# Routed expert blocks begun while the last two pairs of the graph part are still in their stages, and a pair of row blocks every three slots

## Chip, cores and metric

One Trainium2 chip, one NeuronCore of it. The metric is the device time of one execution in microseconds (us), median of the runs shown. Engines are called as in the profile: PE is TensorE, DVE VectorE, ACT ScalarE, POOL GpSimd, SP the SyncE queue.

## What is computed

6,250 nodes with 256 features, 206,250 directed edges sorted by destination. Two graph layers and a projection, then a mixture of 8 experts of which each node takes 2:

```
h6 = relu(segment_sum((ln(x) @ W6)[src] * norm, dst) + b6)
h7 = relu(segment_sum((h6 @ W7)[src] * norm, dst) + b7)
x  = x + h7 @ Wp + bp
xn = ln(ln(x)) * gamma + beta;  logits = xn @ Wr + br;  two largest, softmax weights w
y  = sum over the two experts e of w_e * (gelu(xn @ W1[e] + b1[e]) @ W2[e] + b2[e])
out = x + y
```

All arithmetic that the change touches is float32; `norm` comes from the summed edge weights of the two ends.

## The kernel before

**Layer 1** ends at about 1880 us of the span. Nothing in it is touched.

**Layer 2** runs over numbered slots, from one list that all engines follow (`layer2_slots`). The first 720 of the edge tiles are applied as 24 dense chunks of 3.3 MB, one chunk over four slots, so slots 0 to 95 hold dense matmuls (line 1722). The other tiles are 112 groups of 8, one group a slot in slots 0 to 111 (`L1_GROUPS`): POOL gathers eight times 128 rows with an indirect DMA (`gathers`, line 805) into a ring of four groups, PE sums them (`sums`, line 1736), ACT copies the sum (`copy_sums`, line 1443), PE combines it with the group before (`combine`, lines 1746 and 1748), ACT copies that (`copy_rows`), and SP stores it to `zsum`. POOL may not gather group n before PE has summed group n-4.

**Pairs.** The nodes lie in 25 pairs of 128-row blocks. When its sums are complete, a pair goes through four stages, one a slot (`pair_stage`, `stage_of`, `stage_first`, `stage_last`): stage 0 loads the sums (`zrow<-zsum`), scales and transposes them (lines 1143, 1756) and projects them (line 1768); stage 1 adds the residual and normalizes twice on DVE (`residual_and_norms`); stage 2 transposes (line 1781), computes logits (line 1791) and routes (`router`, with a tanh on ACT, line 1515); stage 3 ranks the rows by expert, works out each row's place in the list of its expert (`places`, its last instruction line 1224) and adds the second bias (line 1812; `first_output`, line 1228). `pair_starts` gives a pair its first slot; the next starts at least `PAIR_SLOTS` = 4 slots later, so no slot holds two pairs. The last starts are 93, 97, 101, 105, 109, 113 and 117; there are 121 slots.

**Sends.** POOL writes each pair's rows to their places in `sorted_x` with four indirect DMAs (`send`, line 813), one a slot, behind the gathers of that slot, 7 slots after the stage (`SEND_LAG`). Each waits until the one before has landed and until the pair is `placed`.

**Experts.** After the last pair has been sent, SP fills the ends of the experts' lists with padding (lines 770 to 774), DVE builds the list of 105 blocks of 128 rows (`block_table`), and the blocks follow one another (`experts`, `block_T`, `block_up`, `block_down`, `block_gelu`, `block_out`): SP loads the rows of block j (line 781), PE transposes them (line 1853), ACT scales (line 1549), DVE copies the block's weights out of the eight experts' (lines 1277, 1284), PE multiplies up (line 1863), ACT applies gelu (line 1559), PE multiplies down (line 1873), ACT weights the rows (line 1567), and POOL adds them to `acc` with an accumulating indirect DMA (line 852). That add waits for the landing of the add before:

```
for j in range(BLOCKS):
    pool.wait_ge(y_ready, j + 1)
    if j:
        pool.wait_ge(y_added, 16 * j)
```

PSUM results of blocks j and j+1 lie in two banks each (`ps_xe`, `ps_h`, `ps_y`). At last SP copies `acc` to the output.

Of the kernel before, what the change touches and what calls it, by code (L numbers as in the profile page):

```python
# [41 lines left out]
PAIR_SLOTS = 4  # L42
# [3 lines left out]
BLOCKS = 105  # L46
SEND_LAG = 7
# [29 lines left out]
def gnn_moe_kernel(nc, A):  # L77
# [32 lines left out]
    with ExitStack() as ctx:  # L110
# [54 lines left out]
        first_of = sb("first_of", [P, NE])  # L165
# [88 lines left out]
        def taker(first, last):  # L254
# [3 lines left out]
            def take(*shape):  # L258
# [8 lines left out]
                if len(shape) == 3:  # L267
# [35 lines left out]
        w2_sb = moe(NE, HC * D)  # L303
        w1_e = moe(2, KD, H)
# [12 lines left out]
        passed, jumps = (w1_e[:, i].rearrange("p k h -> p (k h)").rearrange("p (e j) -> p e j", e=NE)  # L317
                         for i in range(2))
# [34 lines left out]
        ps_b2 = split(bank[5][:, :], PT)  # L353
# [71 lines left out]
        LOADED = 10  # L425
        TABLE0_PARTS = X_LOADS
# [115 lines left out]
        STAGE_AT = {slot + s: (i, b, s) for i, (slot, b) in enumerate(STARTS) for s in range(PAIR_SLOTS)}  # L542

        def layer2_slots(f):

            for n in range(SLOTS):
                c, j = n // 4, n % 4
                f(n, c if c < CHUNKS else None, j, n if n < L1_GROUPS else None, STAGE_AT.get(n))
# [5 lines left out]
        def _(sp):  # L554
# [104 lines left out]

            bad = flag(sp)  # L660
            with sp.If(bad < 1):
# [43 lines left out]
                def layer2_slot(n, c, j, g, stage):  # L705
                    if stage and stage[2] == 0:
                        i, b, _ = stage
# [17 lines left out]
                    if stage and stage[2] == PAIR_SLOTS - 1:  # L725
                        store_acc(stage[0], stage[1])

                layer2_slots(layer2_slot)
            with sp.Else():
# [38 lines left out]
            sp.wait_ge(sent, 16 * 2 * PT * NPAIR)  # L768
            sp.wait_ge(pay0_made, 1)
            sp.dma_start(sorted_x[FILL:FILL + P, :], pay0[:, :]).then_inc(filled, 16)  # L770
            sp.wait_ge(counted, 1)
            for e in range(NE):
                end = sp.value_load(fill_i[0:1, e:e + 1], min_val=0, max_val=FILL)
                sp.dma_start(sorted_x[bass.ds(end, P), :], pay0[:, :]).then_inc(filled, 16)
# [1247 lines left out]
```

## Time and profile before

| | us |
|---|---|
| median of 3 runs | 3775.18 (3773.27 to 3778.09) |
| the profiled execution | 3771.15 |
| its span in the trace | 3769.3 |
| first gather of layer 2 | 1875.91 |
| last gather of layer 2 | 3129.72 |
| last pair placed | 3215.53 |
| first and last add of a block to `acc` | 3256.18 and 3742.8 |

Times of single instructions are counted from the start of the span. The profiled execution lies 4.0 us under the median and 1.9 us above its own span.

### The profile page before, as it was taken

To read this page: it belongs to the slowest core of one execution; us is meant where nothing else is said; L and a number is where in the kernel's file an instruction comes from. 1 tells how busy PE (TensorE), PEld (TensorE's weight loads), DVE (VectorE), ACT (ScalarE), POOL (GpSimd) and SP (SyncE) were. 2 spreads that over 40 slices of the span, in tenths; PEclk is the share of its full clock that TensorE was granted. 3 is DMA by queue.
4 is the path that set the end of the run, shared out by engine and by line. 5 is a ranking of instruction groups with operands and counts; after the bars stand their busy time and mean duration, and the time that the engine had idled before them with its cause. 6 is when DMAs were issued, how large, how long until landed. Compare 5 with 4: busy or idle time off the path is not lost.

```text
span 3769.3 us, 58587 instructions
## 1 busy us (share of the span) xinstructions
PE 2954.2 (78%) x17257; PEld 2010.3 (53%) x17257; DVE 1995.1 (53%) x7494; ACT 1383.3 (37%) x3705; POOL 1993.6 (53%) x2006
## 2 busy tenths in 40 slices
PE   4577289988999999996588888888988664588885
PEld 3456145555555555553355565555655422477775
DVE  7999886777676777751202333333433354333332
ACT  5577355555555555542301111111111110344443
POOL 0000177655555566666277777777777773233332
PEclk9979699999999999998889999888988765799998
DMA  3001355555445555557456666666666642233334
GB/s 102 0 18 36 90 168 164 163 162 164 152 135 162 161 164 165 162 175 232 121 166 211 202 202 200 202 200 201 197 200 201 214 124 72 56 58 58 58 58 106
DMA packets 208606, 535.63 MB, mean 142 GB/s; under 512 B 42924, under 2 KB 138436, under 8 KB 202052
## 3 DMA queue, kind: packets, MB, share of 16 engines
q0 software_dynamic: 105936, 263.26, 28.1%
q1 hardware_dynamic: 99796, 253.82, 19.3%
q10 hardware_dynamic: 2592, 15.16, 1.0%
q8 instruction: 131, 2.15, 0.2%
q14 instruction: 151, 1.24, 0.1%
HBM read 380.42 MB, written 158.05 MB: 143 GB/s over the span
## 4 chain that ended last, share of the span: by engine, by line
PE 38%; DVE 20%; DMA 16%; issue 10%; ACT 7%; POOL 6%; DVEq 2%; SPq 1%; ACTq 0%; POOLq 0%
PE bank L1722 15%; DMA acc<-arena 8%; PE bank L1714 6%; POOL arena L805 6%; DMA zrow<-zsum 5%; ACT arena L1452 3%; DVE arena L942 3%; PE bank L1748 3%; PE bank L1746 3%; PE bank L1736 2%; ACT arena L1460 2%; DMA zsum<-zc 2%; PE bank L1768 2%; PE bank L1863 2%; DVE arena L1112 1%
## 5 line engine op out<-in xcount | busy, mean ns | idle before, releaser
L805 POOL DMA_INDIRECT arena<-table,src_i x1792 | 1723.6, 962 | 843.2 <-issue 514.3
L1722 PE MATMUL bank<-arena 128*128 128x257 f32 x4704 | 1215.6, 394 | 5.5 <-ACT zcd L1469 5.5
L1722 PEld LDWEIGHTS bank<-arena 128*128 128x128 f32 x4704 | 876.7, 196 | 227.6 <-issue 103.4
L1460 ACT ACTIVATE arena<-arena 128x128 bf16<-128x128 bf16 x1440 | 482.4, 393 | 295.9 <-DVE arena L1094 293.6
L1714 PE MATMUL bank<-arena 128*128 128x343 bf16 x2160 | 441.7, 314 | 187.3 <-ACT arena L1460 144.6
L1112 DVE TENSOR_TENSOR arena<-arena,bank 128x343 f32 x720 | 365.7, 508 | 346.9 <-PE bank L1714 266.0
L1714 PEld LDWEIGHTS bank<-arena 128*128 128x128 bf16 x2160 | 180.7, 97 | 428.4 <-issue 199.8
L852 POOL DMA_INDIRECT acc<-arena x105 | 167.8, 1598 | 347.0 <-ACT arena L1567 240.2
L1736 PE MATMUL bank<-arena,s_all 128*32 128x257 f32 x3584 | 265.3, 417 | 70.3 <-DMA arena<-table,src_i 55.5
L1686 PE MATMUL bank<-arena 128*128 128x150 bf16 x1616 | 188.6, 276 | 112.5 <-DVE arena L942 108.9
L1863 PE MATMUL bank<-arena 128*128 128x128 f32 x1680 | 221.3, 286 | 63.8 <-DVE arena L1277 63.6
L1443 ACT COPY zs<-bank 128x257 f32<-128x257 f32 x224 | 83.4, 372 | 504.6 <-PE bank L1736 490.9
L1122 DVE TENSOR_TENSOR arena<-iota_f,rel 128x256 bf16<-128x256 f32 x224 | 93.9, 419 | 301.0 <-PE bank L1748 274.6
L1863 PEld LDWEIGHTS bank<-arena 128*128 128x128 f32 x1680 | 204.1, 198 | 81.6 <-DVE arena L1277 81.3
L1449 ACT COPY zc<-bank 64x257 f32<-64x257 f32 x224 | 82.4, 368 | 444.3 <-PE bank L1748 417.3
L796 POOL PARTITION_ALL_REDUCE bad_all<-bad_f x1 | 0.4, 382 | 441.3 <-DVE bad_f L1084 441.3
L1094 DVE TENSOR_SCALAR arena<-iota_b,arena 128x128 bf16<-128x128 bf16 x720 | 230.6, 320 | 0.0
L1686 PEld LDWEIGHTS bank<-arena 128*128 128x128 bf16 x1616 | 143.1, 117 | 160.0 <-DVE arena L942 156.1
L1092 DVE TENSOR_SCALAR arena<-iota_key,arena 128x343 bf16<-128x343 bf16 x720 | 226.8, 315 | 0.0
L1873 PE MATMUL bank<-arena 128*128 128x256 f32 x840 | 203.2, 386 | 0.0
L1736 PEld LDWEIGHTS bank<-arena,s_all 128*32 128x32 f32 x3584 | 99.1, 116 | 191.5 <-issue 96.1
L1093 DVE TENSOR_SCALAR arena<-iota_b,arena 128x128 bf16<-128x128 bf16 x720 | 187.9, 261 | 0.0
(216 smaller groups left out, 3416.1 us busy)
## 6 DMA issues: line engine op xcount, KB each, us to landing
chunks<-arena SPq DMA_DIRECT2D x24, 3307.5 KB
arena<-chunks SPq DMA_DIRECT2D x22, 3307.5 KB, 13.3
arena<-table,src_i POOLq DMA_INDIRECT x1792
zsum<-zc SPq DMA_DIRECT2D x224, 64.2 KB
arena<-sorted_x SPq DMA_DIRECT2D x105, 132.5 KB, 2.1
zrow<-zsum SPq DMA_DIRECT2D x50, 257.0 KB, 4.4
arena<-in_W ACTq DMA_DIRECT2D x16, 512.0 KB, 13.5
arena<-chunks ACTq DMA_DIRECT2D x2, 3307.5 KB, 19.4
```

Source lines behind the costliest of these rows:

```text
L805: pool.indirect_dma_start(gat[:, r, j, :], None, table[L], bass.IndirectOffsetOnAxis(ap=src_i[:, col:col + 1], axis=0)).then_inc(gathered[ ...
L1092: dve.tensor_scalar(ohk[:, r], iota_key[:, 0:KEYS], key[:, t:t + 1], None, ALU.is_equal)
L1093: dve.tensor_scalar(ohl[:, r], iota_b[:, :], lo_f[:, t:t + 1], None, ALU.is_equal)
L1094: dve.tensor_scalar(parts[:, r, 0], iota_b[:, :], lo_f[:, t:t + 1], w3f[:, 0, t:t + 1], ALU.is_equal, ALU.mult).then_inc(onehot_made, 1)
L1112: dve.tensor_tensor(win, win, ps_b[t % 2].rearrange("p (h w) -> p h w", w=TW), ALU.add).then_inc(added, 1)
L1460: last = act.activation(parts[:, r, i], ohl[:, r], ACT.Copy, scale=w3f[:, i, t:t + 1])
L1686: last = pe.matmul(ps_do, oh_lo[:, r, j // TI, :, j % TI], whi[:, r, j // TI, :, :, j % TI].rearrange("p i n -> p (i n)"), start=False, st ...
L1714: last = pe.matmul(ps_b[t % 2], parts[:, t % OH_RING, i], ohk[:, t % OH_RING], start=(i == 0), stop=(i == 2))
L1722: last = pe.matmul(ps_ap, adj[:, c % 2, h, 0:P], xp[:, h], start=(h == 0), stop=(h == XB_ALL - 1))
L1736: last = pe.matmul(ps_seg[q * WIN:(q + 1) * WIN, :], s_mat[:, r, q * TQ + j], gat[:, r, q * TQ + j], start=(j == 0), stop=(j == TQ - 1))
L1863: last = pe.matmul(ps_h[j % 2][:, c], w1_e[:, j % 2, k, c * P:(c + 1) * P], xeT[:, j % 2, k], start=(k == 0), stop=(k == KD - 1))
L1873: last = pe.matmul(ps_y[j % 2], hs[:, j % 2, c], w2_e[:, j % 2, c], start=(c == 0), stop=(c == HC - 1))
```

## The change

1. `PAIR_EVERY` = 3: pairs may start three slots apart. A slot can hold stage 3 of one pair and stage 0 of the next. The last starts are then 88, 93, 96, 99, 102, 105, 111 and 114, with 118 slots. Nine of the 25 starts move; before slot 93 those are 24, 81 and 89, each to one slot earlier.
2. Sends are issued two behind the gathers of one slot and two behind those of the next, from 5 slots after the start of the pair. Only the first send of a pair waits for the sends before it; the last pair keeps every wait.
3. When 23 pairs are placed (slot 108), DVE lists the experts' whole blocks (`list_whole`): 85 of the 105 are sure to exist by then. Slots 112 to 117 hold two blocks each beside the stages of the last two pairs (`tail_slot` on PE): 12 blocks (`FRONT`). SP loads the first three at slot 112 (`first_blocks`). DVE copies the weights of a slot's two blocks ahead of the pair's stage, and POOL adds them.
4. After slot 117 DVE lists the other 20 blocks (`list_rest`); the padding is written between the loads of blocks 40 to 47 in place of ahead of block 0.
5. PSUM: `ps_xe` and `ps_y` have one bank each; `ps_b2` shares a bank with `ps_proj`.

The core of the diff:

```diff
-PAIR_SLOTS = 4
+PAIR_SLOTS, PAIR_EVERY = 4, 3
-BLOCKS = 105
-SEND_LAG = 7
+BLOCKS, LATE_PAIRS, PER_SLOT, FILL_FROM = 105, 2, 2, 40
+SEND_LAG = 5
-        ps_xe = [split(bank[6 + i][:, 0:KD * P], KD) for i in range(2)]
-        ps_h = [split(bank[2 + i][:, :], HC) for i in range(2)]
-        ps_y = [bank[4 + i][:, 0:D] for i in range(2)]
+        ps_xe = split(bank[0][:, 0:KD * P], KD)
+        ps_h = [split(bank[i][:, :], HC) for i in (2, 5)]
+        ps_y = bank[1][:, 0:D]
-                slot += PAIR_SLOTS
+                slot += PAIR_EVERY
+        WHOLE = ceil_div((NPAIR - LATE_PAIRS) * PT * P * 2 - NE * (P - 1), P)
+        FRONT = PER_SLOT * (SLOTS - L1_GROUPS)
+        LISTED_AT = STARTS[NPAIR - LATE_PAIRS - 1][0] + PAIR_SLOTS - 1
# SP
+            def first_blocks():
+                sp.wait_ge(counted, 1)
+                sp.wait_ge(sent, 16 * 2 * PT * (NPAIR - LATE_PAIRS))
+                for j in range(XB_RING):
+                    load_block(j)
+                    if n == L1_GROUPS:
+                        first_blocks()
+                    for j in blocks_at(n):
+                        load_block(j + XB_RING)
# POOL
-                for n in range(SLOTS + SEND_LAG):
-                    if n < L1_GROUPS:
-                        gathers(1, n)
-                    turn = STAGE_AT.get(n - SEND_LAG)
-                    if turn:
-                        i, _, q = turn
-                        send(i, i % 2, q)
+                for n in range(L1_GROUPS):
+                    gathers(1, n)
+                    for i, half in SENDS_AT[n]:
+                        for q in range(half * PT, half * PT + PT):
+                            send(i, i % 2, q)
+                for n in range(L1_GROUPS, SLOTS):
+                    for j in blocks_at(n):
+                        add_block(j)
+                    for i, _, s in STAGES_AT[n]:
+                        if s == PAIR_SLOTS - 1:
+                            for q in range(2 * PT):
+                                send(i, i % 2, q)
# DVE
+                if n == L1_GROUPS:
+                    weights_ready()
+                if n >= L1_GROUPS:
+                    experts(blocks_at(n))
+                for i, b, s in stages:
                     pair_stage(i, b, s, i % 2, i // 2, i - 1 if i > 1 else None)
+                if n == LISTED_AT:
+                    list_whole()
...
+            list_rest()
+            dve.wait_ge(counted, 2)
+            experts(range(FRONT, BLOCKS))
# PE
+            def tail_slot(n, stages):
+                first, second = blocks_at(n)
...
+                block_step(first)
+                for i, _, s in stages[:-1]:
+                    stage_first(i, i % 2, s)
+                    stage_last(i, s)
+                for i, _, s in stages[-1:]:
+                    stage_first(i, i % 2, s)
+                block_step(second)
+                for i, _, s in stages[-1:]:
+                    stage_last(i, s)
```

## Rows read from the trace of the kernel before

**Rows 1.** The page: busy us, share of the span and instructions of all engines.

```profile
PE 2954.2 (78%) x17257; PEld 2010.3 (53%) x17257; DVE 1995.1 (53%) x7494; ACT 1383.3 (37%) x3705; POOL 1993.6 (53%) x2006
```

**Rows 2.** Busy time by stretch: all engines, granted clock, DMA share, GB/s.

```profile
2400.00:2990.00 590.00, 495.64 (x2660) 333.16 (x2652) 221.49 (x1026) 67.73 (x182) 447.71 (x463) 0.90 0.63 196
2990.00:3131.00 141.00, 86.00 (x401) 40.72 (x401) 59.51 (x268) 18.84 (x50) 101.00 (x105) 0.58 0.56 163
3131.00:3256.00 125.00, 42.00 (x175) 29.47 (x176) 55.90 (x248) 14.58 (x38) 17.41 (x17) 0.56 0.18 53
3256.00:3742.00 486.00, 415.39 (x2674) 369.84 (x2673) 168.17 (x510) 237.75 (x719) 166.24 (x104) 0.97 0.37 57
```

**Rows 3.** Timeline of POOL in layer 2: gathers, sends, idle before.

```profile
2532.56 0.99 POOL L813 DMA_INDIRECT sorted_x<-arena  x1 [1.28 <-DMA sorted_x<-arena]
...
2658.75 1.05 POOL L813 DMA_INDIRECT sorted_x<-arena  x1 [0.30 <-issue]
2660.10 0.97 POOL L805 DMA_INDIRECT arena<-table,src_i  x1 [0.30 <-issue]
...
3017.39 0.97 POOL L805 DMA_INDIRECT arena<-table,src_i  x1 [8.54 <-PE bank L1736]
...
3129.72 0.94 POOL L805 DMA_INDIRECT arena<-table,src_i  x1 [0.30 <-issue]
```

**Rows 4.** Timeline, DVE and ACT: one pair placed; the last group's sum copied.

```profile
2670.98 0.17 DVE L1224 CAST arena<-arena 128x4 int32<-128x4 f32 x1
...
3136.19 0.38 ACT L1443 COPY zs<-bank 128x257 f32<-128x257 f32 x1 [3.46 <-PE bank L1736]
```

**Rows 5.** The chain that ended last, 2990 to 3256: start, us, what.

```profile
3011.87 3.73 PE bank L1768 x8
...
3027.29 1.11 PE bank L1781 x4
...
3039.89 0.70 DVE arena L1228
3041.10 4.33 DMA zrow<-zsum
...
3078.83 4.91 DMA zrow<-zsum
...
3158.97 3.80 PE bank L1768 x8
...
3243.61 2.19 DMA arena<-sorted_x
```

**Rows 6.** All adds of blocks: duration, first and last start.

```profile
L852 POOL DMA_INDIRECT acc<-arena x105: 1551/1551/2018, 3256.2 to 3742.8; - x105
```

**Rows 7.** Timeline inside one block of the steady run.

```profile
3504.58 0.47 ACT L1567 ACTIVATE arena<-bank,arena 128x256 f32<-128x256 f32 x1 [0.59 <-PE bank L1873]
...
3505.37 2.05 PE L1863 MATMUL bank<-arena 128*128 128x128 f32 x16 [0.61 <-DVE arena L1277]
...
3507.26 1.89 PE L1873 MATMUL bank<-arena 128*128 128x256 f32 x8
```

**Rows 8.** Timeline, several engines, around the tail.

```profile
3190.45 0.97 POOL L813 DMA_INDIRECT sorted_x<-arena  x1 [2.66 <-DMA sorted_x<-arena]
3193.71 0.97 POOL L813 DMA_INDIRECT sorted_x<-arena  x1 [2.29 <-DMA sorted_x<-arena]
...
3219.90 0.17 DVE L1254 CAST arena<-next_of 128x8 int32<-128x8 f32 x1 [2.15 <-issue]
...
3229.49 0.23 DVE L1270 TENSOR_SCALAR arena<-arena 128x128 int32<-128x128 f32 x1
...
3246.40 3.75 PE L1863 MATMUL bank<-arena 128*128 128x128 f32 x16
...
3247.40 1.28 ACT L1559 ACT_TABLE_LOAD   x1
...
3478.89 0.69 DVE L1277 COPY arena<-arena 128x1024 f32 x1 [2.33 <-issue]
```

More of the change, by code:

```diff
@@ L316, in gnn_moe_kernel @@
         jump = moe(NE)
-        passed, jumps = (w1_e[:, i].rearrange("p k h -> p (k h)").rearrange("p (e j) -> p e j", e=NE)
-                         for i in range(2))
+        taken = moe(NE)
+        list_from = moe(NE + 1)
         first_f = moe(P)
@@ L1239, in pair_stage, with layer2_slot @@
                     first_output(i)
-            def layer2_slot(n, c, j, g, stage):
+            def layer2_slot(n, c, j, g, stages):
                 if n + 1 < L1_GROUPS:
@@ L1292, in block_weights, with experts_of, weights_ready @@
                 dve.tensor_copy(row_e[:, j % XB_RING], xe[:, j % XB_RING, PAY - 1:PAY]).then_inc(cols_made, 1)
-            def experts():
+            def experts_of(blocks):
+                _, of = nc.values_load_multi_w_load_instructions(
+                    exp_i[0:1, blocks[0]:blocks[-1] + 1], [mybir.EngineType.DVE], min_val=0, max_val=NE - 1,
+                    skip_runtime_bounds_check_because="exp_i is clamped to 0..7 where it is made")
+                return of
+            def weights_ready():
                 dve.wait_ge(counted, 1)
@@ L1297, in experts @@
                 dve.wait_ge(w2_in, 16 * NE)
-                for j in range(BLOCKS):
-                    if j % LOADED == 0:
-                        _, of = nc.values_load_multi_w_load_instructions(
-                            exp_i[0:1, j:min(j + LOADED, BLOCKS)], [mybir.EngineType.DVE], min_val=0, max_val=NE - 1,
-                            skip_runtime_bounds_check_because="exp_i is clamped to 0..7 where it is made")
-                    block_weights(j, of[j % LOADED])
+            def experts(blocks):
+                for j in blocks:
+                    if (j - blocks[0]) % LOADED == 0:
+                        of = experts_of(blocks[j - blocks[0]:][:LOADED])
+                    block_weights(j, of[(j - blocks[0]) % LOADED])
             def slow_layer(L):
@@ L1528, in stage_of, with layer2_slot @@
                     weights_T(i)
-            def layer2_slot(n, c, j, g, stage):
+            def layer2_slot(n, c, j, g, stages):
                 if j == 0 and 0 < n <= 4 * (CHUNKS - 1):
@@ L1548, in block_T @@
                 for k in range(KD):
-                    last = act.activation(xeT[:, j % 2, k], ps_xe[j % 2][:, k], ACT.Identity, bias=bec[:, k:k + 1],
+                    last = act.activation(xeT[:, j % 2, k], ps_xe[:, k], ACT.Identity, bias=bec[:, k:k + 1],
                                           scale=gac[:, k:k + 1])
@@ L1829, in stage_last, with layer2_slot @@
                     second_bias(i)
-            def layer2_slot(n, c, j, g, stage):
+            def layer2_slot(n, c, j, g, stages):
+                if n >= L1_GROUPS:
+                    return tail_slot(n, stages)
                 steps = range(SLOT_STEPS[j], SLOT_STEPS[j + 1]) if c is not None else range(0)
@@ L1838, in layer2_slot @@
                     apply_step(1, c, step)
-                if stage:
-                    stage_first(stage[0], stage[0] % 2, stage[2])
+                for i, _, s in stages[:1]:
+                    stage_first(i, i % 2, s)
                 if g is not None:
```

226 lines of the change are left out of this document (147 added, 79 removed).

## The prediction, made before the changed kernel had run

> **What bounds the kernel now.** I read the busy line first, for what it does not say. PE is busy 78% of the span and POOL 53% [rows 1]: an average over stages with other limits. So I cut the end of the program into stretches [rows 2]. To 2990 us PE is busy 84% (495.64 of 590) at full clock; from 2990 to 3131 its busy share is 61% and the granted clock 0.58; from 3131 to 3256 it is 34%, at 0.56, and POOL is nearly idle; from 3256 to 3742 PE is busy 85% at 0.97. The third stretch, 125 us in which no engine is busy even half the time, is where a change can find time.
>
> Then the timeline of POOL in layer 2, because the busy share understates it. A gather or send is shown as 0.95 to 1.05 us with 0.30 us of "issue" before it [rows 3], so POOL is taken 1.25 to 1.30 us by each. 896 gathers and the sends among them fill 1875.9 to 3131 almost without a gap: besides two waits of a send for a landing (the 1.28 us one is shown, the other is 1.5), I find one stop, 8.54 us at 3017.39, for PE to give back a ring buffer [rows 3]. The reader is to see that POOL is as good as full for 1255 us. PE with its pairs keeps nearly the same pace: two queues are level here, and what is won in one comes out only as far as the other allows.
>
> After the gathers the chain of waits shows the pairs one by one: load of the sums at 3041.10 and at 3078.83, 37.7 us for one pair [rows 5]. Inside one pair: projection ends 3015.6, next transposes 3027.3, so 11.7 us of normalizing on DVE; the output ends 3040.6 [rows 5]. The last two pairs run alone, then sends, padding and list, and the rows of block 0 are loaded at 3243.61.
>
> In the block part, 105 adds start from 3256.2 to 3742.8 [rows 6]: 486.6/104 = 4.68 us a block. An add waits for the landing of the one before, and I take this as the bound, since POOL starts at a fixed distance after it; PE needs 2.05 us up and 1.89 us down at full clock [rows 7], with transposes about 4.3, and is close behind.
>
> **Part 1, gathers and sends.** The end of the gathers sets when slot 111 can run. To its last gather POOL now has 90 sends before it, where 83 went before: slots up to 110 cover 22 pairs and a half instead of the stages of slots up to 103. That is 7 x 1.30 = +9.1. What POOL can win is its idle time: 8.54 and 2.8 us [rows 3]. The waits for the landing of each send go, except at a pair's first. But the lag is shorter: the first two sends come 2 slots behind the pair's stage 3, and POOL runs ahead of PE by up to four groups. Look at the pair that started at slot 65 (the thirteenth): its last placing instruction is at 2670.98 [rows 4], while POOL has ended the gathers of slot 70 by 2658.45 and goes on with a send of another pair at 2658.75 [rows 3]. In the new order it would stand there and wait 12.5 us. By the same comparison the three pairs before it are 2.4, 5.0 and 8.4 us late. These are not added: a POOL that has waited is no longer so far ahead. So the cost is between 0 (if the pairs run earlier by more) and 12.5. I take 7.5, because the pair that starts at slot 23 in place of 24 shares its slot with stage 3 of the other, which should bring PE about 5 us forward. Last gather ends: 3130.7 - 8.5 - 2.8 + 9.1 + 7.5 = 3136.0.
>
> **Part 2, a pair every three slots.** The period of a pair from slot 96 becomes: norms 11.7; transposes, combine, logits, router, ranks, bias and output as before, together 3027.3 to 3040.6 = 13.3; then scale 0.7, transposes 1.1, relu 1.1, projection 3.7 = 6.6 [rows 5]; scale and relu are what lies between the shown rows. The sum is 31.6 against 37.7: the load no longer follows the output, as SP issues it one stage earlier. Slot 96 itself also moves forward. Where before the projection of that pair ended at 3015.6, behind a load that landed late among the experts' weights, I expect some 10 to 28 us earlier. Four pairs at 31.6 put the end of stage 3 of slot 108 between 3108 and 3131. POOL's last gather at 3136.0 is then the later one, so most of what the pairs win here is not seen at the end. If the pairs win nothing at slot 96, they, with the 10 us in which DVE makes the list, come last by 5 to 9 us: that is the upper bound.
>
> After the last gather, before: 3130.7, then sum copied 3136.19 [rows 4]: 5.5 us later. Then transposes 1.1, combine 2.1, projection 3.7: the projection of the pair of slot 111 ends at 3136.0 + 5.5 + 6.9 = 3148.4. The same pair's projection ended before at 3158.97 + 3.80 = 3162.8 [rows 5]: 14.4 us won.
>
> **Part 3, the six tail slots.** No row shows such a slot; I add it up along DVE's queue, where two blocks' weights now stand in front of the stage. PE is partly at 1.2 GHz: the first block's multiply up took 3.75 us against 2.05, and before it PE had been idle [rows 8]. A multiply down at that clock I take as 3.5, a little under twice the 1.89 of [rows 7]. I take the slow clock for the first block of a slot after a long wait and the full one for the second. Each slot's call that reads the experts' numbers costs DVE 2.3 us [rows 8], and one weight copy 0.7.
>
> - 112: rows of blocks 0 and 1 arrive and are copied, 5.5; norms 11.7: 17.2.
> - 113: 2.3 + 0.7, up 3.75, down 3.5, transposes of the pair and block 1.5, up 2.05, down 1.9, logits 0.8, router 3.5 with one table load: 20.0.
> - 114: 2.9 + 3.75 + 3.5; ranks and bias 2.2, output and scale 1.4, transposes 1.0, up and down 3.95, projection 1.7: 20.4.
> - 115: up and down of one block, 4.3, copies 1.8, norms 11: 17.1.
> - 116: as 113, 20.3.
> - 117: 2.9 + 3.75 + 3.5 + 0.4 + 2.05 + 1.9 + bias 1.1 + output 0.7 = 16.3.
>
> Together 111 us. With PE at full clock throughout it is 98, at 1.2 GHz throughout 137. The stages of these two pairs alone took from 3162.8 to 3217.8, 55 us: 12 blocks, worth 56.2, cost about 56 more. So **the interleaving by itself wins nothing**; the gain is what stood between the last pair and block 0.
>
> ACT switches between gelu and tanh four times more. The trace has 1.28 us for a table load [rows 8], so 5.1 us, half of it on the path and in the sum. *The Trainium skill (ScalarE: Activation LUTs, What ACT_TABLE_LOAD costs) gives 2.66 us a switch, with a drain behind the load. This case shows the load alone; by the page the slots would be up to 5.5 us longer together.*
>
> **Part 4, after slot 117.** DVE lists the rest. Before, the list took from 3219.9 to 3229.9 [rows 8], 10 us in some 20 steps, of which four go over 1024 elements, now 160: between 4 and 10, and I take 6.3. Then 2.3 + 0.7 to the weights of block 12, up 3.75, down 3.5, ACT and POOL 1.1: add 11 starts 17.7 after the last output. POOL then sends the last pair with every wait. Sends stood 3.3 us apart [rows 8], up to 4.4; four of them and the return to the add are 12.4. Add 12 starts 30.1 after the output. Nothing covers this: adds are the bound. The padding (now beside blocks 40 to 47) costs nothing: SP has some 3.5 us free in each 4.68 us block.
>
> **The sum.** Add 12 now: 3148.4 + 111 + 30.1 = 3289.5. Before: 3256.2 + 12 x 4.68 = 3312.3. From there both have 93 blocks and the same end. Won: 22.8; I round to 22. The profiled execution, 3771.15, becomes 3749; the median lies 4.0 above it, 3753.
>
> **The rivals.**
>
> *PE stays at 1.2 GHz through the tail.* For: the granted clock is 0.56 to 0.58 from 2990 to 3256 [rows 2], with PE busy 34 to 61%. Against: with two blocks a slot PE is busy more like 70%. Price: tail 137 in place of 111, +26: 3779, about **no change**, and within 0.2% also if a few of the blocks run faster. 0.14.
>
> *The tail is serial, and the kernel slower.* In a slot, DVE's copy for its second block waits for PE's multiply down of the block two before, which waits for ACT's gelu, which waits for the up; only then does DVE turn to the pair. If each block passes wholly ahead of the stage (rows, up, gelu, down at the slow clock, about 10 us), a slot costs 20 more than its stage, 6 x 20 + 55 = 175: +64 on my 111, and the median is 3817; with half of it, 3785. It decides when the six slots take over 134 us, 22 each. Against: DVE's norms, 11.7 us, lie beside both blocks on PE. 0.13.
>
> *POOL gives nothing away and the clock is high.* Placed stalls 0 and tail 98: 7.5 + 13 more, 3733, and some more if add 11 comes sooner. 0.15.
>
> *One bank each for `ps_xe` and `ps_y` slows every block.* A multiply down now waits for ACT's copy of the block just before. In the steady run that copy ends at 3505.05 and the next down starts at 3507.26 [rows 7]: 2.2 us to spare. If it did bite, one 0.47 us copy a block is 93 x 0.47 = +44: 3797. 0.05. [...]
>
> *My forecast,* 3740 to 3766, has the rest: 0.53.
>
> **How the numbers follow.** 3753 is the likeliest. The range takes in the fast case at 3727 (its price with a little room) and the slow clock and half of the serial tail up to 3786. A measurement of this kernel tells about 0.2%, 7.5 us, from no change. Faster: 0.53 and 0.15 and a small part of the slow clock, 0.70. Same: most of the slow clock and a mild serial tail, 0.13. Slower: serial tail and single bank, 0.17.
>
> **What would show it.** Right: last gather at 3129 to 3141; pair loads 32 us apart after slot 96; first add near 3160; the list of the rest begun near 3260; add 12 near 3290, then 4.68 us a block. Wrong: long waits of POOL's sends for the placing of a pair in layer 2, a last gather after 3145, six tail slots over 134 us, or a period over 4.8 us in the long run of blocks.

## The result, and the profile after

The changed kernel takes **3744.3 us**, the median of 9 runs (3729.38 to 3749.6), beside 3767.11 for the kernel before in the same series (9 runs, 3755.57 to 3778.09). The ratio is 0.9939, 95% interval 0.9921 to 0.9958: faster by 0.6%. Forecast were 3753 and 22 us won; measured are 22.8 us won between the medians, and 26.8 between the two profiled spans (3769.3 and 3742.5). The measured median lies 8.7 us under the 3753 because the kernel before came out lower as well: 3767.11 over 9 runs, where the forecast started from 3775.18 over 3. The gain is as forecast. Two terms of its sum are not, and the experiments are mostly about them. Later series on other chips gave the same kernel 13.5 us won, and once 180 us lost.

The page's busy line of the changed kernel, which answers to [rows 1]: every engine is busy for the same time as before within 0.3%.

```profile
PE 2960.6 (79%) x17257; PEld 2016.0 (54%) x17257; DVE 1995.9 (53%) x7522; ACT 1381.2 (37%) x3705; POOL 1992.6 (53%) x2006
```

Busy time by stretch, changed kernel, the columns of [rows 2], cut at its own last gather, last output and last add:

```profile
2400.00:2990.00 590.00, 504.77 (x2696) 339.25 (x2696) 222.79 (x1030) 68.42 (x184) 434.67 (x452) 0.90 0.64 195
2990.00:3148.00 158.00, 91.99 (x426) 44.44 (x426) 79.62 (x360) 19.97 (x53) 117.34 (x121) 0.59 0.55 156
3148.00:3254.00 106.00, 72.01 (x396) 61.24 (x396) 47.23 (x203) 34.72 (x100) 22.55 (x17) 0.77 0.28 57
3254.00:3716.00 462.00, 379.48 (x2425) 339.12 (x2424) 157.77 (x490) 214.82 (x650) 154.35 (x98) 0.95 0.36 59
```

The second stretch, to the last gather, has become longer, 158 us against 141. The third is what the change is about. In 106 us PE is busy 68% at a granted clock of 0.77; before it was 125 us with PE busy 34% at 0.56. The block part behind it is shorter because 12 blocks are already done. (The prediction calls the clock of the first stretch full; its granted clock is 0.90 on the mean, before and after.)

All adds of blocks, changed kernel, which answers to [rows 6]: the first starts at 3172.0 in place of 3256.2, the last at 3716.3 in place of 3742.8.

```profile
L863 POOL DMA_INDIRECT acc<-arena x105: 1552/1552/2031, 3172.0 to 3716.3; - x105
```

The same path in both profiles, in us of the span. "24th projection" is that of the pair one before the last, with which my Part 2 ends.

| | before | forecast | after |
|---|---|---|---|
| last gather starts | 3129.72 | 3135 | 3148.09 |
| 24th projection ends | 3162.8 | 3148.4 | 3162.9 |
| last pair's output ends | 3217.8 | 3259.4 | 3254.8 |
| add 12 starts | 3313.23 | 3289.5 | 3285.41 |
| last add starts | 3742.75 | | 3716.3 |

The reader sees three things. Layer 2 has won nothing in this profile: the 24th projection ends where it ended before. The tail is 19 us shorter than forecast (91.9 against 111). And from the output to add 12 the forecast of 30.1 meets 30.6.

**Where layer 2 lost it.** Timeline of POOL, changed kernel: the last of the seven waits of a send for a placing, and the last gather.

```profile
3029.09 1.00 POOL L854 DMA_INDIRECT sorted_x<-arena  x1 [4.20 <-DVE arena L1275]
...
3148.09 0.95 POOL L844 DMA_INDIRECT arena<-table,src_i  x1 [0.30 <-issue]
```

What POOL waited for in all, changed kernel (us, times, longest):

```profile
POOL sorted_x L854 <- DVE arena L1275: 23.9, 7, 4.7
```

Line 1275 is the last instruction of `places`. Seven sends stood there for 1.9 to 4.7 us each, 23.9 us together, and every gather behind them came later by that. Five profiles with this same order of gathers and sends (this one and those of after_third, sends_spread, list_late and no_front below) bear it out: their sends waited 23.9, 8.5, 4.5, 27.6 and 21.6 us, first to last gather took 1271.9, 1257.8, 1254.3, 1273.8 and 1268.5 us, and the difference is 1246 to 1250 in all five. PE felt it at the last two groups. Timeline of PE, changed kernel:

```profile
3138.49 1.94 PE L1839 MATMUL bank<-arena,s_all 128*32 128x257 f32 x16 [6.23 <-DMA arena<-table,src_i]
...
3154.12 1.94 PE L1839 MATMUL bank<-arena,s_all 128*32 128x257 f32 x16 [11.04 <-DMA arena<-table,src_i]
...
3159.14 3.78 PE L1871 MATMUL bank<-arena,hT 128*128 128x256 f32 x8
```

So the pairs were ready first, as the forecast had it, and their gain is not seen at the end. That they did gain is in SP's timeline of the changed kernel, where `zrow<-zsum` loads the sums of one pair after another:

```profile
3026.04 0.39 SPq L646 DMA_DIRECT2D zrow<-zsum  x1
...
3056.95 0.39 SPq L646 DMA_DIRECT2D zrow<-zsum  x1
...
3088.72 0.39 SPq L646 DMA_DIRECT2D zrow<-zsum  x1
```

30.9 and 31.8 us a pair; before 37.7 [rows 5], forecast 31.6.

**Where the tail was quicker.** Timeline of DVE, changed kernel, from the first weights of block 0 to the list of the rest: line 1356 and line 1363 are the two weight copies of a block, line 970 ends a norm, line 1279 is the last pair's output.

```profile
3152.81 0.69 DVE L1356 COPY arena<-arena 128x1024 f32 x1 [0.45 <-issue]
...
3175.66 0.74 DVE L970 TENSOR_SCALAR arena<-arena,mv,rv 128x256 f32<-128x256 f32 x2
3176.37 0.69 DVE L1356 COPY arena<-arena 128x1024 f32 x1
...
3190.52 0.69 DVE L1356 COPY arena<-arena 128x1024 f32 x1 [0.56 <-issue]
...
3197.97 0.69 DVE L1363 COPY arena<-arena 128x1024 f32 x1 [5.28 <-PE bank L1999]
...
3225.11 0.69 DVE L1356 COPY arena<-arena 128x1024 f32 x1
...
3241.65 0.69 DVE L1356 COPY arena<-arena 128x1024 f32 x1 [0.56 <-issue]
...
3254.15 0.69 DVE L1279 TENSOR_TENSOR arena<-arena,bank 128x512 f32<-128x512 f32 x1 [3.12 <-PE bank L1915]
...
3264.80 0.69 DVE L1356 COPY arena<-arena 128x1024 f32 x1 [2.50 <-issue]
```

Reading the experts' numbers of a slot's two blocks stops DVE for 0.45 to 0.56 us or not visibly at all; the 2.3 us of [rows 8] come where the kernel reads the numbers of ten blocks in one call, and the 2.50 us before the first block of the rest show that again. The copies of block 0 stand at 3152.81, before the 24th projection, so slot 112 begins with the norms. PE's multiplies up (line 1989) in slot 113, chain of waits of the changed kernel (start, us, what):

```profile
3177.11 3.39 PE bank L1989 x16
...
3182.89 1.79 PE bank L1989 x16
```

And of slots 113 and 114, timeline of PE: line 1999 is the multiply down, first in slot 113, then up and down in slot 114.

```profile
3180.34 1.89 PE L1999 MATMUL bank<-arena 128*128 128x256 f32 x8
...
3191.27 3.78 PE L1989 MATMUL bank<-arena 128*128 128x128 f32 x16 [3.80 <-DVE arena L1356]
3194.84 2.97 PE L1999 MATMUL bank<-arena 128*128 128x256 f32 x8
```

In slots 113, 114, 116 and 117 the first block goes up at the slow clock for most or all of its time (3.39, 3.78, 3.78 and 3.79 us), behind 3.8 to 9.7 us in which PE waited, and the second, 5.6 to 11.1 us later, at the full one (1.95 us; 2.64 in slot 114). That was my assumption, and for the first ups it holds in the four slots to which the sum applies it; in slots 112 and 115 the first block goes up in 1.95 us. For the downs it holds less: those of the same four first blocks took 1.89, 2.97, 2.74 and 3.00 us, where the sum had 3.5 each. The clock came back during them or before.

### The profile page after: what moved, and what is told of

Read it like the earlier page. It is cut to its first block and busy times, and to the rows that moved or that the text cites. A ratio compares the mean times of both kernels' runs of the same rounds, so it can differ in the third digit from the quotient of the medians.

```text
span 3742.5 us, 58552 instructions
## 1 busy us (share of the span) xinstructions
PE 2960.6 (79%) x17257; PEld 2016.0 (54%) x17257; DVE 1995.9 (53%) x7522; ACT 1381.2 (37%) x3705; POOL 1992.6 (53%) x2006
## 3 DMA queue, kind: packets, MB, share of 16 engines
q0 software_dynamic: 105936, 263.26, 28.5%
## 5 line engine op out<-in xcount | busy, mean ns | idle before, releaser
L1839 PE MATMUL bank<-arena,s_all 128*32 128x257 f32 x3584 | 269.6, 423 | 106.1 <-DMA arena<-table,src_i 91.2
L1145 DVE TENSOR_SCALAR arena<-iota_b,arena 128x128 bf16<-128x128 bf16 x720 | 232.4, 323 | 0.0
L1657 ACT ACTIVATE arena<-bank,arena 128x128 f32<-128x128 f32 x420 | 119.7, 368 | 204.7 <-PE bank L1989 204.7
## 6 DMA issues: line engine op xcount, KB each, us to landing
arena<-in_W ACTq DMA_DIRECT2D x16, 512.0 KB, 16.5
arena<-chunks ACTq DMA_DIRECT2D x2, 3307.5 KB, 19.1
```

Source lines behind the costliest of these rows:

```text
L1145: dve.tensor_scalar(parts[:, r, 0], iota_b[:, :], lo_f[:, t:t + 1], w3f[:, 0, t:t + 1], ALU.is_equal, ALU.mult).then_inc(onehot_made, 1)
L1839: last = pe.matmul(ps_seg[q * WIN:(q + 1) * WIN, :], s_mat[:, r, q * TQ + j], gat[:, r, q * TQ + j], start=(j == 0), stop=(j == TQ - 1))
```

## Experiments

Each ratio is to the kernel before, run on the same chip in the same series. The kernels of one series stand together. Single executions of one kernel differ by up to 29 us and each kernel has one profile, so profiles are compared by stretches and totals by medians. The changed kernel itself was not run in the first series. Every experiment computes all that the reference asks.

### First series: one part at a time (kernel before 3757.69, 23 runs)

**A longer lag for the early pairs** (lag7_early). Is the waiting of the sends what layer 2 lost?

```diff
+        def lag_of(i):
+            return SEND_LAG + 2 if STARTS[i][0] < 93 else SEND_LAG
```

> The changed kernel with one edit: pairs that start before slot 93 are sent 7 and 8 slots after their start, as before the change, in place of 5 and 6; the others keep 5 and 6. In the changed kernel POOL stands 23.9 us in seven waits for a pair to be placed (six of them, 19.7 us, at pairs that start before slot 93), and its last gather starts at 3148.1, against 3129.7 before the change. Theory A (POOL is full to the last gather, so a wait of it comes out at the end): six waits go, last gather at 3130 to 3133, total 15 to 18 us less, about 3728. Theory B (PE with its pairs sets the end, and a waiting POOL only loses its lead): last gather moves by less than 5 us, total within 3 us of 3744. If the two are level, something between: 5 to 12 us.

Measured: 3740.47, ratio 0.995 (0.9931 to 0.9968). The waits of the early pairs are gone, and one has come up in their place. Timeline of POOL, this kernel:

```profile
3020.04 1.00 POOL L857 DMA_INDIRECT sorted_x<-arena  x1 [13.18 <-DVE arena L1278]
```

This is the pair of slot 96, which still has the short lag and sits among the loads of the experts' weights. POOL, no longer held up before, arrived 13 us early. The last gather starts at 3138.61. The waits do cost time, but taking out the early ones mostly moves them: 13.2 us are left of 23.9, the last gather is 9.5 us earlier, and the total can't be told from that of the changed kernel (0.9939, and 0.9953 below).

**The list of the rest later** (list_late). DVE lists the last 20 blocks behind block 31 and not right after the last output.

```diff
+            experts(range(FRONT, 32))
             list_rest()
             dve.wait_ge(counted, 2)
-            experts(range(FRONT, BLOCKS))
+            experts(range(32, BLOCKS))
```

> The changed kernel with one edit: the second list is built after block 31 in place of after the last tail slot (the first list already names blocks 0 to 84). Theory A: the 7 us of the list stand alone between the last output and block 12, no add runs beside them, so they come out; in the run of blocks DVE is one block ahead, which hides some 4.7 of the 7 us: total 4 to 5 us less, about 3740. Theory B: the list is hidden already by the four sends of the last pair, which POOL makes before add 12: no change.

Measured: 3742.7, ratio 0.9953 (0.9937 to 0.9969). From the last output to add 12 it is 26.6 us in place of 31.3 (from the output's start), 4.7 less. But from add 16 to add 40, where the list now lies, it is 118.35 against 112.8: 5.6 more. The adds are a chain without slack for 6 us of DVE, so in these profiles the list costs as much in the one place as in the other.

**The last pair's sends spread** (sends_spread). One send behind each of the adds 12 to 15, in place of four ahead of add 12.

```diff
-                        if s == PAIR_SLOTS - 1:
+                        if s == PAIR_SLOTS - 1 and i < NPAIR - 1:
...
+                for q in range(2 * PT):
+                    add_block(FRONT + q)
+                    send(NPAIR - 1, (NPAIR - 1) % 2, q)
```

> The changed kernel with one edit: the four sends of the last pair go one by one behind the adds of blocks 12 to 15 in place of all four between adds 11 and 12. In the changed kernel add 11 starts near 3271.8 and add 12 at 3285.4. Theory A (the serial sends stand in the way of add 12): add 12 starts 5 to 9 us after add 11, total 5 to 8 us less, about 3737. Theory B (block 12 itself isn't ready sooner, or the sends' writes slow the adds by as much): at most 2 us less.

Measured: 3725.82, ratio 0.9915 (0.99 to 0.993). Timelines of POOL. First the changed kernel, in which add 12 (3285.41) waits behind four sends:

```profile
3271.60 1.55 POOL L863 DMA_INDIRECT acc<-arena  x1 [15.22 <-ACT arena L1665]
3273.46 0.99 POOL L854 DMA_INDIRECT sorted_x<-arena  x1 [0.31 <-issue]
3277.16 0.98 POOL L854 DMA_INDIRECT sorted_x<-arena  x1 [2.71 <-DMA sorted_x<-arena]
3280.70 0.96 POOL L854 DMA_INDIRECT sorted_x<-arena  x1 [2.56 <-DMA sorted_x<-arena]
3284.14 0.96 POOL L854 DMA_INDIRECT sorted_x<-arena  x1 [2.49 <-DMA sorted_x<-arena]
3285.41 1.60 POOL L863 DMA_INDIRECT acc<-arena  x1 [0.30 <-issue]
```

Then this kernel, in which each send fills the wait of an add:

```profile
3247.96 1.55 POOL L863 DMA_INDIRECT acc<-arena  x1 [15.18 <-ACT arena L1668]
3252.43 1.55 POOL L863 DMA_INDIRECT acc<-arena  x1 [2.92 <-DMA acc<-arena]
3254.29 1.32 POOL L854 DMA_INDIRECT sorted_x<-arena  x1 [0.31 <-issue]
3256.99 1.57 POOL L863 DMA_INDIRECT acc<-arena  x1 [1.38 <-DMA acc<-arena]
```

Add 12 follows add 11 after 4.47 us and not 13.81, and from add 12 to 16 it is 19.3 us against 18.4. The sends are hidden: 9.3 us less from the last output to add 12, 8.4 of them still there at add 16. The total is down by more than the 5 to 8 us expected: 3725.82 is 14.7 and 16.9 us under its two neighbours above, and the profile accounts for 9 of these. Its interval lies below that of list_late (0.9937 to 0.9969).

**No blocks in the tail slots** (no_front). The first blocks come after the last slot. The other parts stay: a pair every three slots, the list in two parts, the padding late.

```diff
-        FRONT = PER_SLOT * (SLOTS - L1_GROUPS)
+        FRONT = 0
...
-            return range(PER_SLOT * (n - L1_GROUPS), PER_SLOT * (n - L1_GROUPS + 1)) if n >= L1_GROUPS else range(0)
+            return range(0)
```

> The changed kernel without its interleaving: no block runs in slots 112 to 117; the rows of the first three blocks are loaded after the last slot, and all 105 blocks follow. Pairs every three slots, the sends and the two lists stay. The prediction held that 12 blocks in the tail slots cost as much as they win, and that only what stood between the last pair and block 0 was saved: then this kernel is within 3 us of the changed one (3744). The trace of the changed kernel says otherwise: its six slots took 90 us from the projection of the 24th pair to the last output, where the two pairs alone took 55 before the change, so 12 blocks cost 35 us and are worth 56; then this kernel is 15 to 25 us slower than the changed one, 3760 to 3770, about as slow as before the change.

Measured: 3747.26, ratio 0.9967 (0.9955 to 0.998): 10.4 us won with no block interleaved, where the changed kernel has 22.8 and 13.5 in its two series on quick chips. The 3760 to 3770 that its tail seemed to promise did not come; the total lies within 3 us of the 3744.3, as the prediction's sentence on the interleaving has it. By stretches, in us:

| | before | no_front | after |
|---|---|---|---|
| 24th projection to last output (start) | 54.3 | 50.9 | 91.2 |
| last output to add 0 | 39.1 | 22.3 | |
| 24th projection to add 12 | 150.4 | 128.5 | 122.5 |

21.9 of the 27.9 us are won without the interleaving: 16.8 from what no longer stands between the last pair and block 0, 3.4 in the last two pairs, which now lie closer, 1.7 in the first twelve adds. The interleaving adds 6, for these reasons: the twelve blocks would take 55.3 us behind the pairs and make the tail 40.3 longer, but then the four sends and the second list stand between the last output and add 12, and there it is 31.3 us where no_front has 22.3 to add 0. Three more profiles with blocks in the tail have 121.7 to 123.1 us from the 24th projection to add 12, so the 6 us are not an accident of one; in the medians (ratios 0.9967 against 0.9953 and 0.9939, intervals that overlap) they can't be told.

### Second series: another chip (kernel before 4291.11, 11 runs)

All kernels were slower here. The four variants that were run all have the short lag, and all are slower than the kernel before.

**The changed kernel again** (after_again), with no edit.

> The changed kernel as it is, a second time, to stand beside the others of this chip. Theory: ratio to the kernel before 0.992 to 0.997. Single executions of one kernel lie up to 25 us apart, much of it in layer 2 (its gathers took 1254 to 1274 us in four traces whose layer 2 has the same instructions), so a profile's sections are compared, and totals only by their medians.

Measured: 4470.97, ratio **1.0428** (1.0402 to 1.0454), where 0.992 to 0.997 was expected. What POOL waited for in all, this run of the changed kernel:

```profile
POOL sorted_x L854 <- DVE arena L1275: 331.7, 22, 21.1
```

331.7 us where the other chip had 23.9. The adds keep their period (4.694 us from add 16 to the last), the tail its length (90.8 to the start of the last output, 91.2 there) and the output its 30.9 us to add 12. Layer 2, first gather to last, takes 1711.7 us in place of 1271.9. Besides the sends, POOL stops here for other things too: 29.8 us in nine stops for PE to give back a ring buffer and 107.2 in 29 for which the profile names no engine; on the other chip there was none of either.

**The kernel before, with the lag of 5** (before_lag5): the one line, nothing else.

```diff
-SEND_LAG = 7
+SEND_LAG = 5
```

> The kernel before with one number changed: sends from 5 slots after the start of a pair in place of 7. Theory A (POOL's last gather sets the end of layer 2 also before the change): POOL waits 12 to 20 us for placings, the last gather comes that much later, and the total is 10 to 20 us more. Theory C (before the change the pairs set the end, 33 us from last gather to the projection of the 24th pair; only with pairs three slots apart, 15 us, does POOL set it): POOL waits the same 12 to 20 us, the last gather comes up to 15 us later, and the total stays within 5 us of the kernel before.

Measured: 4472.3, ratio 1.043 (1.0402 to 1.0459), the same as the whole change. Waits of POOL, this kernel; some 290 us are more than the usual 0.30 us before each, and for them the profile names no releaser:

```profile
POOL sorted_x L813 <- issue: 314.1, 86, 16.3
```

So in this series the lag by itself accounts for the loss. The 12 to 20 us of waits that were expected were far off.

**Pairs four slots apart, no blocks in the tail** (every4_no_front): as no_front, with

```diff
-PAIR_SLOTS, PAIR_EVERY = 4, 3
+PAIR_SLOTS, PAIR_EVERY = 4, 4
```

> As no_front (no block in the tail slots), and pairs again at least four slots apart, as before the change; sends, lists and padding stay changed. Theory C: the pairs set the end of layer 2 again; from the last gather to the projection of the 24th pair 30 us or more against 14.8 in no_front, while the last gather comes up to 8 us earlier, since fewer sends lie before it; pairs that run one by one cost 3.4 us more at the last output. Together 10 to 20 us slower than no_front. Rival: POOL and pairs are level in both, and the starts are worth less than 5 us.

Measured: 4481.39, ratio 1.0449 (1.0424 to 1.0475). Up to the last gather its sends waited 294.8 us for the placing. The pair spacing is not the cause of this chip's loss, and what the spacing is worth in the total can't be told under it. The first half of theory C shows all the same: from the last gather to the 24th projection it is 42.2 us, and 20.9 in pad_first below, whose pairs are three slots apart. But the last gather lies 15.4 us earlier than there, and the projection only 5.9 us later.

**Padding first** (pad_first): no_front with the nine padding stores and the second list ahead of the rows of block 0.

```diff
                 layer2_slots(layer2_slot)
+                pad_ends()
                 first_blocks()
```

> As no_front, with one more edit: the nine padding stores go ahead of block 0, behind the last send and the second list, as before the change. Theory: the stretch between last output and first add is what the change saved. It took 39 us before and 22.3 us in no_front; with the padding ahead it is 37 to 41 again, and the kernel 14 to 18 us slower than no_front, at the level of the kernel before or a little above. Rival: the list and the weights are late anyway, and it costs under 6 us.

Measured: 4494.73, ratio 1.0488 (1.0459 to 1.0516). From the last output to add 0 it is 38.0 us; in every4_no_front of the same chip 22.1, in the kernel before 39.1. That is the whole of the gap: 16 us that stood ahead of block 0 and need not. The list is the short one in this kernel too, so the 16 us belong to the padding and its wait for the list, and not to the list's length. no_front itself was not run on this chip; the totals of pad_first and every4_no_front differ by 13.3 us, but their pairs lie differently too.

### Third series: a third chip, the lag, and a better version (kernel before 3760.19, 23 runs)

**The changed kernel a third time** (after_third), with no edit.

> The changed kernel itself, once more, as the yardstick for the other kernels of this comparison. Theory A (the short lag of the sends loses little where the placing of a sum, at most 5 us late in the changed kernel's trace, is nearly in time): ratio 0.992 to 0.998 on a chip on which the kernel before takes near 3760 us, with POOL's waits for the placing at 15 to 40 us in all. On a chip on which it takes near 4290 us: ratio 1.04 to 1.05 again, with waits of some 300 us. Theory B (the ratio of the slow chip was an accident of that execution series): there ratio 0.99 to 1.00.

Measured: 3746.71, ratio 0.9953 (0.9934 to 0.9972). In its profile only three sends wait for a placing, 8.5 us in all (expected were 15 to 40), and the last gather starts at 3135.01. Timeline of POOL, this run:

```profile
3135.01 0.95 POOL L844 DMA_INDIRECT arena<-table,src_i  x1 [0.30 <-issue]
```

The 24th projection ends at 3147.4. These are the forecast's numbers (3136.0 for the gather's end, 3148.4), in another execution of the same program; it was the quickest of its 12.

**The kernel before with the lag of 5 again** (lag5_second), on a quick chip.

> The kernel before with its lag of seven slots cut to five, nothing else. The last pair's sends lie in slots of the tail, so a shorter lag could bring its rows two slots nearer the front, but each send may stand before a placing that isn't done. Theory A (on a quick chip the lag costs only the waits, some 24 us of POOL, that the gathers then inherit, and wins nothing on the path because POOL is the bound of layer 2): last gather 5 to 20 us later than with seven slots, ratio 1.001 to 1.006. Theory B (the lag is a gain there, the pairs' own path being the bound): ratio 0.992 to 0.998. On a chip on which the kernel before takes near 4290 us both theories expect 1.04 to 1.05, as measured there once.

Measured: 3767.53, ratio 1.0008 (0.9994 to 1.0021): no difference that can be told, and neither theory's interval, though nearer to A. The last gather starts 5.3 us later than in [rows 3] (2.2 of it because layer 2 began later), the 24th projection ends at 3162.4 as before. Five of the sends waited 16.9 us up to the last gather, without a named releaser, as on the slow chip. Here 27.3 us pass from the last gather to the projection, so the gathers are not last, and their delay is hidden.

**Lags by place, weights spread** (lags_weights).

```diff
+        def lag_of(i):
+            return SEND_LAG + (2 if STARTS[i][0] < 93 else 1 if STARTS[i][0] < 105 else 0)
...
-                    load_experts()
+                    act.wait_ge(applied[1], SLICES * CHUNKS)
+                if 4 * CHUNKS <= n < 4 * CHUNKS + NE:
+                    load_expert(n - 4 * CHUNKS)
```

> The changed kernel with the lag of seven slots for pairs that start before slot 93, six for those from 93 to 104 and five after them, and with the sixteen transfers of the experts' weights issued two a slot over slots 96 to 103 in place of all at slot 96. Theory A (the one wait of 13 us for the pair of slot 96, seen when only the early pairs had seven slots, came from the short lag and from the weights' transfers in its way): that wait is gone, POOL's waits for the placing fall from 23.9 us to under 8, last gather of layer 2 8 to 16 us earlier than in the changed kernel of the same chip, ratio to the kernel before 0.990 to 0.994 against 0.995 for the changed kernel. Theory B (layer 2 has its pace from the gathers' own transfers, and a wait that goes comes back elsewhere): ratio within 0.0015 of the changed kernel's. On a chip on which the kernel before takes near 4290 us: theory A expects 1.00 to 1.01 in place of 1.043, theory B over 1.03.

Measured: 3736.91, ratio 0.9929 (0.9907 to 0.9951). The sends' waits for the placing are down to 2.3 us in this profile. In their place POOL stops five times, 10.6 us in all, for PE to give back a ring buffer, which it never did in the changed kernel: part of the wait has come back elsewhere, as theory B has it. The last gather starts at 3138.97, later than the 3135.01 of the changed kernel beside it, where theory A wanted 8 to 16 us less. The wait of 13 us at the pair of slot 96 is gone; whether by its longer lag or by the spread weights isn't separated. The ratios differ by 0.0024 with intervals that overlap. It stays open whether this part wins anything on a quick chip; on the slow one it wasn't run, so whether it mends the loss there is not known.

**The same with the sends spread** (best2): both edits together.

> The kernel of the lags and the spread weights with, in addition, the four sends of the last pair each behind one block's add (blocks 12 to 15) in place of four together ahead of block 12. Theory A: the four sends' 8 to 9 us leave the stretch between the last output and add 12, as they did when this was tried alone (21.9 us against 31.3), so 4 to 10 us below the kernel without it, ratio to the kernel before 0.985 to 0.990 on a quick chip. Theory B (the adds behind them are the path, and each send then delays them by as much): add 16 to the end comes out as late, ratio within 0.001 of the kernel without it. On a chip on which the kernel before takes near 4290 us the difference to the kernel without it is the same 4 to 10 us under theory A.

Measured: 3720.63, ratio **0.9892** (0.9869 to 0.9916). This beats both kernels: its interval lies below that of the changed kernel beside it. Out to add 12 is 22.1 us against 31.1 without the spread sends, add 12 to 16 is 18.6 against 18.3. The profile accounts for 9 of the 16 us between the two medians; 4 to 10 were expected. On the slow chip this kernel wasn't run either. Timeline of POOL, this kernel:

```profile
3256.27 1.55 POOL L866 DMA_INDIRECT acc<-arena  x1 [14.78 <-ACT arena L1673]
3260.94 1.55 POOL L866 DMA_INDIRECT acc<-arena  x1 [3.12 <-DMA acc<-arena]
3262.80 1.12 POOL L857 DMA_INDIRECT sorted_x<-arena  x1 [0.30 <-issue]
3265.45 1.57 POOL L866 DMA_INDIRECT acc<-arena  x1 [1.54 <-DMA acc<-arena]
```

## Why the prediction was right, step by step

**Part 1, the sends' waits: mis-sized in the profile after.** Forecast were 7.5 us between 0 and 12.5; measured 23.9, and the last gather ended 13 us late (3149.0 for 3136.0). The step that failed is "These are not added: a POOL that has waited is no longer so far ahead". Six pairs in a row from 2433 to 2676 waited 1.9 to 4.7 us each: POOL gathers quicker than the pairs advance and has its lead back by the next pair, so a small wait comes again at nearly every one. The upper bound should have been the sum of the latenesses (28.3 us for the four pairs that the prediction names). Other executions of the same layer 2 waited 4.5, 8.5, 21.6 and 27.6 us, and its time from first to last gather follows that, 1254.3 to 1273.8 us. So my term is a draw from a spread and 7.5 lies inside it; why one execution waits 4.5 us and another 27.6 on the same chip stays open.

**Part 2, a pair every three slots: right.** 30.9 and 31.8 us for 31.6, gathers last, and 13.9 us from the end of the last gather to the end of the projection for 12.4.

**Part 3, the tail: too long by 19.1.** Slot by slot, from DVE's rows above (a slot begins with the weights' copy or the norms; 114 ends with the projection at 3208.5):

| slot | 112 | 113 | 114 | 115 | 116 | 117 |
|---|---|---|---|---|---|---|
| forecast | 17.2 | 20.0 | 20.4 | 17.1 | 20.3 | 16.3 |
| measured | 13.5 | 14.2 | 18.0 | 16.6 | 16.5 | 13.2 |

Four terms of the sum were mis-sized. Where a slot reads numbers, my 2.3 was 0.56 or nothing: about 8 us over the four. In slot 112 the 5.5 us for the rows of blocks 0 and 1 weren't on the path, as the first copies had been made before the projection ended and what remained was mostly the norms: 3.7. The four first downs were set at 3.5 us each and took 10.6 together and not 14.0: 3.4. And the step "ACT switches between gelu and tanh four times more" failed: the sum holds half of 5.1 us for it, and no such switch took place. Both kernels have four table loads in the whole execution, and the changed one has a single load in the tail, at 3166.00; the tanh of the router, line 1605, runs among the gelus without one. That is 2.6. Together these are some 17.7 of the 19.1 us; the rest stays open. Timeline of ACT, changed kernel:

```profile
3166.00 1.28 ACT L1657 ACT_TABLE_LOAD   x1
3167.29 1.14 ACT L1657 ACTIVATE arena<-bank,arena 128x128 f32<-128x128 f32 x4
...
3187.98 0.20 ACT L1605 ACTIVATE arena<-arena 128x2 f32<-128x2 f32 x1 [1.07 <-DVE arena L1231]
```

The load takes the 1.28 us of [rows 8], and the gelu follows 0.01 us behind it. The Trainium skill (ScalarE: Activation LUTs, What ACT_TABLE_LOAD costs) has a drain there; this row does not show one. "The interleaving by itself wins nothing" is nearly right: by no_front's profile it has 6 us of 28. But the reason given, that the tail grows by the 56 us that the blocks are worth, is not: it grew by 40, and 9 more went to the sends and the list behind it.

**Part 4: right.** 30.6 for 30.1, add 11 at 16.8 after the output's end for 17.7, add 12 another 13.8 behind it for 12.4, then 4.69 us a block (from add 16 to the last) for 4.68; the first two of these offset each other. The late padding shows no cost: from add 40 to add 56 a block takes 4.73 us, and 4.72 before.

**The sum.** +14.5 to the 24th projection, -19.1 in the tail, +0.5 behind it: add 12 came 4.1 us before its forecast. The two errors are of opposite sign, and a right total with these behind it is partly luck in this profile. In after_third only the tail's is left (92.6 us), and the execution is quicker than forecast: its span is 3727.0. The median of its series lies at 3746.71, which no single profile explains.

**The signs.** The prediction named a last gather after 3145 and long waits of the sends for a placing as signs that it is wrong; the gather came at 3148.09 and the waits were 23.9 us. By its own signs the path through layer 2 was wrong in this profile, and the right total doesn't mend that. Add 0, expected near 3160, came at 3171.97, and in after_third at 3159.9. The list of the rest began at 3257 for 3260.

**The rivals.** *PE at 1.2 GHz:* no, 0.77 in the tail. *Serial tail:* no, 91.9 us, far from the 134 at which it decides; DVE's norms lie beside the blocks. *Fast case:* its tail (98) yes and more, its free sends no. *Single banks:* no, the period is 4.69 against 4.67 from add 16 to the last. The single banks, and the sends without a wait for the one before, have no run of their own. What I had not thought of at all is that the short lag could make the kernel 4.3% slower on another chip.

## What to carry over

When one engine is held up by another for a few microseconds at one point, ask how soon it has its lead back: if within one round, the wait counts once in every round. And a lag that looks idle on one chip may carry another, so it is tried on more than one before it is cut. Before work is interleaved into a gap, remove or hide what stands serially in it: here the late padding gave 16 us and four spread sends 9, the interleaving of twelve blocks 6.

## What was not expected of the hardware

- Chips differed by 14% on the same program: each series ran on a chip of its own, and the kernel before takes 3757.69, 4291.11 and 3760.19 on the three. There was one series on the slow chip, so it isn't separated whether the chip or its condition at that time was slow. The parts with much transfer are slower: the untouched layer 1 ends 272 us later (first gather of layer 2 at 2148.26 for 1876.15), and layer 2 takes 1711.7 for 1271.9, of which, by the totals, some 180 come from the short lag. The block part is not (4.69 us a block on both). The page gives the queue of indirect transfers the same time in all, 24.0% of 4460.1 against 28.5% of 3742.5, so it isn't shown that single packets are slower; what holds these stretches up stays open, the more so as no trace of the kernel before was taken on that chip. Granted clock and PE's busy share are lower there too (0.80 and 71% from 2200 to 3700, for 0.88 and 82% from 1900 to 3100 in the changed kernel's first profile); which is cause and which effect is open.
- Why the shorter lag costs 180 us there and next to nothing elsewhere is argued only. Shown is this: the last eight dense chunks of layer 2, each for four slots, are loaded 62.8 us apart there and 44.6 in the changed kernel's first profile, and 22 sends waited up to 21.1 us each where 1 to 10 waited up to 5.5 in the five profiles above. The reading is that PE is later against POOL at each pair, so each send waits, and each wait delays the gathers for which PE waits in turn.
- Reading the experts' numbers of two blocks stops DVE 0.45 to 0.56 us or not visibly, a call for ten blocks or for the list 2.1 to 2.5 us.
- A tanh between two gelus needs no table load in this kernel: four loads in the whole execution before and after, although the two functions alternate in the tail.
- Executions of one program spread by 29 us (3728.78 to 3757.57), and in the profiles layer 2 alone by 20, which the waits of the sends account for.
